# An image tower on one core: the causal attention's selection and softmax cut at the last visible key, and the last attention cut in two halves

## What is computed

```python
def L2_attn(x, Wq, Wk, Wv, Wo):            # the causal attention: 4 heads of 16
    scores = jnp.max(Q[:, :, :, None, :] + K[:, :, None, :, :], axis=-1)
    scores = jnp.where(causal_mask, -jnp.inf, scores)
    topk_vals, topk_idx = jax.lax.top_k(scores, 8)
    attn = jax.nn.softmax(topk_vals, axis=-1)
    ctx = jnp.einsum('bhtk,bhtkd->bhtd', attn, V gathered at topk_idx)
    return ctx @ Wo.T

def L3_attn(nodes, W):                     # the last attention: one head of 64
    x = jnp.einsum('bnf,fg->bng', nodes, W)
    prods = jnp.einsum('bnf,bmf->bnm', x, nodes)
    att_scores = jax.nn.softmax(prods / sqrt(64), axis=-1)
    return jnp.einsum('bnm,bmf->bnf', att_scores, nodes)
```

## Time and profile before

| | |
|---|---|
| Median of 3 runs | 168.89 us (168.25 to 169.76) |
| The profiled execution's own time | 169.38 us |
| Its span in the profile | 167.5 us |
| PE busy | 148.9 us (89%) |
| DVE busy | 102.5 us (61%) |
| ACT busy | 71.7 us (43%) |
| POOL busy | 32.3 us (19%) |
| PE's granted clock, mean | 0.988 |

### The profile page before, as it was taken

How to read it: one execution, slowest core, us unless ns; L and a number is a source line. 1 busy time by engine, 2 the same in 40 slices (tenths; PEclk the granted TensorE clock), 3 DMA queues, 4 the chain that set the end, 5 groups by cost and what they waited for, 6 DMA issues and landing times.

```text
span 167.5 us, 2891 instructions
## 1 busy us (share of the span) xinstructions
PE 148.9 (89%) x1122; PEld 72.0 (43%) x1122; DVE 102.5 (61%) x284; ACT 71.7 (43%) x133; POOL 32.3 (19%) x83
## 2 busy tenths in 40 slices
PE   6999889989997997988998896999799998999970
PEld 2446265534542352534543312466335454564420
DVE  7314876844657629487497799932868466213981
ACT  3736942756362010365430000615574056476523
POOL 7400000037778400001000000700039200000000
PEclk9999999999999999999999996999999999999999
DMA  5999960000000000000032000000000000000001
GB/s 171 328 429 319 301 244 0 4 0 2 2 6 0 0 0 0 0 4 0 0 56 54 0 0 2 0 4 0 0 4 0 0 0 4 0 0 4 2 0 35
DMA packets 4916, 8.26 MB, mean 49 GB/s; under 512 B 2747, under 2 KB 2875, under 8 KB 4774
## 3 DMA queue, kind: packets, MB, share of 16 engines
q1 hardware_dynamic: 4902, 8.07, 14.9%
HBM read 7.70 MB, written 0.37 MB: 48 GB/s over the span
## 4 chain that ended last, share of the span: by engine, by line
PE 60%; DVE 23%; ACT 8%; DMA 4%; issue 3%; POOL 0%; DVEq 0%; ACTq 0%; POOLq 0%
PE ps L386 9%; PE ps L445 8%; PE ps L432 7%; DVE scores L1280 5%; PE ps L793 5%; PE ps L439 4%; PE ps L393 3%; PE ps L400 3%; DMA k_scratch<-k_parts_tok 2%; DVE scores_rest L1299 2%; PE ps L536 2%; PE ps L544 2%; ACT hidden L855 2%; DMA k_parts_img<-k_scratch 2%; DVE hidden_gated L1090 1%
## 5 line engine op out<-in xcount | busy, mean ns | idle before, releaser
L386 PE MATMUL ps<-idle_operand 128*128 128x512 bf16 x153 | 42.8, 403 | 4.1 <-DVE scores L1280 1.7
L1090 DVE TENSOR_TENSOR hidden_gated<-hidden,ps 128x576 f32<-128x576 f32 x28 | 19.9, 751 | 10.3 <-PE ps L439 8.9
L855 ACT ACTIVATE hidden<-ps,weights_sb 128x576 f32<-128x576 f32 x28 | 19.5, 737 | 12.0 <-PE ps L432 9.5
L386 PEld LDWEIGHTS ps<-idle_operand 128*128 128x128 bf16 x153 | 13.5, 104 | 22.2 <-issue 6.2
L847 ACT ACT_TABLE_LOAD x16 | 20.5, 1283 | 0.3
L835 ACT ACTIVATE squares<-ps 128x288 f32<-128x288 f32 x8 | 3.3, 411 | 33.9 <-PE ps L445 9.2
L445 PE MATMUL ps<-hidden_gated,weights_sb 128*64 128x288 f32 x112 | 16.4, 419 | 0.0
L1029 DVE COPY centred<-ps 128x288 f32<-128x288 f32 x8 | 3.7, 457 | 17.2 <-ACT squares L835 17.2
L432 PE MATMUL ps<-h,weights_sb 64*128 64x288 f32 x80 | 13.0, 436 | 1.1 <-ACT hidden L855 0.8
L300 POOL CAST combine_parts_T<-combine_parts_T 48x288 f32<-48x288 bf16 x3 | 1.3, 421 | 65.2 <-DVE combine_parts_T L1061 65.2
L1280 DVE TENSOR_REDUCE scores<-ps 128x32 f32<-128x512 f32 (+1 forms) x15 | 8.8, 665 | 2.2 <-PE ps L679 2.2
(11 more groups left out here) (284 smaller groups left out, 231.9 us busy)
## 6 DMA issues: line engine op xcount, KB each, us to landing
patch_sb<-patches SPq DMA_DIRECT2D x6, 288.0 KB, 5.4
weights_sb<-weights SPq DMA_DIRECT2D x1, 1108.0 KB, 9.5
weights_sb<-weights SPq DMA_DIRECT2D x1, 717.0 KB, 14.5
weights_sb<-weights SPq DMA_DIRECT2D x1, 689.0 KB, 13.2
weights_sb<-weights SPq DMA_DIRECT2D x1, 640.0 KB, 7.2
weights_sb<-weights SPq DMA_DIRECT2D x1, 512.0 KB, 11.9
weights_sb<-weights SPq DMA_DIRECT2D x1, 394.0 KB, 12.9
weights_sb<-weights SPq DMA_DIRECT2D x1, 375.5 KB, 6.5
```

The costliest lines, as they stand in the source:

```text
L386: mm(PS[:, bank, :], idle_in[:, 0:P], idle_in[:, :], start=True, stop=True)
L855: act.activation(HR[:, at % RING, :, :], two(ZA if ch % 2 == 0 else ZB), func, bias=w(f"b1_{n}")[:, ch:ch + 1]).then_inc(S["act_out"], 1)
L1090: dve.tensor_tensor(HG[:, at % GRING, :, :], HR[:, at % RING, :, :], two(GATE_AT[n][ch]), ALU.mult)\
```

## The change

In the causal attention each query tile is now worked on up to its last visible key: 8, 16, 24, 32 and 40 columns in L1287 and L1299, and 24 and 40 columns in the two pieces of the subtraction, the exponential and the division. The first piece of the subtraction waits for the first 12 of the 20 selections only. The masking multiplication is in two instructions (tiles 0 to 2, tiles 3 and 4), and PE transposes the first three tiles behind the first of them. For the columns that are no longer written, POOL fills all of `probs` (1280 columns in place of 480) and all of `scores_rest` (800 columns, new) at the start.

In the last attention each step is cut by the half h: both matmul loops have h as the outer loop, and the reduction, subtraction, exponential, sum, multiplication and the four transposes of each half are single steps with semaphore counts of their own. The second half's transposed probabilities are copied by DVE, between its two pieces of weight centring, and the first half's by ACT. The fillers ahead of the transposes are 7 in place of 9, and behind them 1 in place of 4.

```diff
+        CUT = ((0, 3, 24), (3, QT, SPAD))
@@ POOL
-            fills = [... (PR[:, :, :, SPAD:64], 0.0), ...
+            fills = [... (PR[:, :, :, :], 0.0), ...
+                     (REP[:, :, :, :], NEG), (ss[:, :], 1.0)]
...
-            pool.wait_ge(S["topped"], QT * HEADS)
-            for a, b in cut:
+            for a, b, keys in CUT:
+                pool.wait_ge(S["topped"], b * HEADS)
                 (subtract, columns 0:keys)
@@ PE
-            pe.wait_ge(S["prob2"], 1)
-            for pair in range(2):
-                z = flat2(ZA if pair == 0 else ZB, QT * P)
-                for j in range(QT):
-                    last = pe.transpose(...)
-                last.then_inc(S["prob2_t"], 1)
+            for n, (a, b, _) in enumerate(CUT):
+                pe.wait_ge(S["prob2"], n + 1)
+                for pair in range(2):
+                    z = flat2(ZA if pair == 0 else ZB, QT * P)
+                    for j in range(a, b):
+                        last = pe.transpose(...)
+                    if n == 1:
+                        last.then_inc(S["prob2_t"], 1)
...
-            for b8 in range(PER):
-                r0 = (b8 % 2) * 64
-                for h in range(2):
+            for h in range(2):
+                for b8 in range(PER):
+                    r0 = (b8 % 2) * 64
                     last = mm(PS[r0:r0 + POS, ZA + h, ...], XT[rows(h), ...], HP[rows(h), ...], ...)
-            last.then_inc(S["s3_done"], 1)
-            idle(9, ZB)
-            pe.wait_ge(S["p3_ready"], 1)
+                last.then_inc(S["s3_done"], 1)
+            idle(7, ZB)
             pe.wait_ge(S["h3_copied"], 1)
-            z = flat2(ZB, 8 * P, POS)
-            for q in range(8):
-                last = pe.transpose(z[:, q * P:(q + 1) * P], E3[:, q, :], c("ident"))
-            last.then_inc(S["p3_t"], 1)
-            idle(4, G)
-            pe.wait_ge(S["p3_copied"], 1)
-            for b8 in range(PER):
-                r0 = (b8 % 2) * 64
-                for h in range(2):
+            for h in range(2):
+                pe.wait_ge(S["p3_ready"], h + 1)
+                for q in range(4):
+                    last = pe.transpose(PS[0:POS, ZB + h, ...], E3[:, 4 * h + q, :], c("ident"))
+                last.then_inc(S["p3_t"], 1)
+            idle(1, G)
+            for h in range(2):
+                pe.wait_ge(S[f"p3_copied{h}"], 1)
+                for b8 in range(PER):
+                    r0 = (b8 % 2) * 64
                     last = mm(PS[rows(h), YB, b8 * POS:(b8 + 1) * POS], HB[:, b8, rows(h)],
                               ET[:, 4 * h + b8 // 2, r0:r0 + POS], start=False, stop=True, ...)
@@ DVE
-                    dve.max(top[:, j, h, :], SC[:, j, h, :]).then_inc(S["topped"], 1)
+                    dve.max(top[:, j, h, :], SC[:, j, h, 0:8 * (j + 1)]).then_inc(S["topped"], 1)
...
+            for h in range(2):
+                dve.wait_ge(S["s3_done"], h + 1)
+                step(dve.tensor_reduce(half3(r3[0], h), s3(h), AX, ALU.max))
+            sync()
+            for h in range(2):
+                dve.tensor_tensor(half3(S3, h), s3(h), row3(r3[0], h), ALU.subtract).then_inc(S["exp3_in"], 1)
+            for h in range(2):
+                dve.wait_ge(S["exp3_out"], h + 1)
+                step(dve.tensor_reduce(half3(r3[1], h), half3(E3, h), AX, ALU.add))
+            sync()
             link(dve.reciprocal(r3[2][:, :], r3[1][:, :]))
+            for h in range(2):
+                dve.tensor_tensor(half3(E3, h), half3(E3, h), row3(r3[2], h), ALU.mult).then_inc(S["p3_ready"], 1)
...
+            centre_wd(0)
+            dve.wait_ge(S["p3_t"], 2)
+            dve.tensor_copy(ET[:, 4:8, :]..., PS[0:POS, ZB + 1, 0:4 * P]).then_inc(S["p3_copied1"], 1)
+            centre_wd(1)
```

More of the change, by code:

```diff
@@ L300, in gates32 @@
                 pool.tensor_copy(CTF[0:6 * E, :], CT3[0:6 * E, :]).then_inc(S["ctf_ready"], 1)
-            fills = [(eps[:, 0:1], EPS), (eps[:, 1:2], EPS * EPS), (ones[:, :], 1.0), (SC[:, :, :, :], NEG), (PR[:, :, :, SPAD:64], 0.0), (VB[:, :, :, :], 0.0),
+            fills = [(eps[:, 0:1], EPS), (eps[:, 1:2], EPS * EPS), (ones[:, :], 1.0), (SC[:, :, :, :], NEG), (PR[:, :, :, :], 0.0), (VB[:, :, :, :], 0.0),
                      (warm[:, :], 0.0), (rr[:, :], 1.0),
-                     (ss[:, :], 1.0)]
+                     (REP[:, :, :, :], NEG), (ss[:, :], 1.0)]
             for n, (t, value) in enumerate(fills):
@@ L354, in _ @@
             pool.tensor_scalar(WRG[:, :], w("Wr"), w("gam2"), None, ALU.mult).then_inc(S["wr_gam"], 1)
[L355 to L359 removed]
+            for a, b, keys in CUT:
+                pool.wait_ge(S["topped"], b * HEADS)
+                pool.tensor_tensor(SE[:, a:b, :, 0:keys].rearrange("p j h s -> p (j h) s"),
+                                   SC[:, a:b, :, 0:keys].rearrange("p j h s -> p (j h) s"),
                                    top[:, a:b, :, 0].rearrange("p j h -> p (j h)").unsqueeze(2)
[L361 removed]
+                                   .to_broadcast([P, (b - a) * HEADS, keys]), ALU.subtract).then_inc(S["sub2"], 1)
             pool.wait_ge(S["top_sum"], 1)
[L363 removed]
+            for n, (a, b, keys) in enumerate(CUT):
                 pool.wait_ge(S["exp2_out"], n + 1)
[L365 to L367 removed]
+                pool.tensor_tensor(SE[:, a:b, :, 0:keys].rearrange("p j h s -> p (j h) s"),
+                                   SE[:, a:b, :, 0:keys].rearrange("p j h s -> p (j h) s"),
+                                   d20[1][:, a * HEADS:b * HEADS].unsqueeze(2).to_broadcast([P, (b - a) * HEADS, keys]),
                                    ALU.mult).then_inc(S["norm2"], 1)
@@ L689, in _ @@
             idle(4, MB)
-            pe.wait_ge(S["prob2"], 1)
-            for pair in range(2):
-                z = flat2(ZA if pair == 0 else ZB, QT * P)
-                for j in range(QT):
-                    last = pe.transpose(z[:, j * P:(j + 1) * P],
-                                        PR[:, j, 2 * pair:2 * pair + 2, :].rearrange("p h s -> p (h s)"), c("ident"))
-                last.then_inc(S["prob2_t"], 1)
+            for n, (a, b, _) in enumerate(CUT):
[3 more added lines that the diff above has]
+                    for j in range(a, b):
+                        last = pe.transpose(z[:, j * P:(j + 1) * P],
+                                            PR[:, j, 2 * pair:2 * pair + 2, :].rearrange("p h s -> p (h s)"), c("ident"))
+                    if n == 1:
+                        last.then_inc(S["prob2_t"], 1)
             idle(3, MB)
@@ L921, in _ @@
             act.activation(TE[:, :, :, :], TE[:, :, :, :], ACT.Exp).then_inc(S["top_out"], 1)
-            for n, (a, b) in enumerate(((0, 3), (3, QT))):
+            for n, (a, b, keys) in enumerate(CUT):
                 act.wait_ge(S["sub2"], n + 1)
-                act.activation(SE[:, a:b, :, :], SE[:, a:b, :, :], ACT.Exp).then_inc(S["exp2_out"], 1)
+                act.activation(SE[:, a:b, :, 0:keys], SE[:, a:b, :, 0:keys], ACT.Exp).then_inc(S["exp2_out"], 1)
             table(ACT.Sqrt)
@@ L950, in _ @@
                .then_inc(S["h3_copied"], 1)
-            act.wait_ge(S["exp3_in"], 1)
-            act.activation(E3[:, :, :], S3[:, :, :], ACT.Exp, scale=float(D) ** -0.5).then_inc(S["exp3_out"], 1)
+            for h in range(2):
+                act.wait_ge(S["exp3_in"], h + 1)
+                act.activation(E3[:, 4 * h:4 * h + 4, :], S3[:, 4 * h:4 * h + 4, :], ACT.Exp, scale=float(D) ** -0.5)\
+                   .then_inc(S["exp3_out"], 1)
             table(ACT.Sqrt)
             act.wait_ge(S["p3_t"], 1)
-            act.activation(ET[:, :, :].rearrange("p q t -> p (q t)"), flat2(ZB, 8 * P, POS), ACT.Copy)\
-               .then_inc(S["p3_copied"], 1)
+            act.activation(ET[:, 0:4, :].rearrange("p q t -> p (q t)"), PS[0:POS, ZB, 0:4 * P], ACT.Copy)\
+               .then_inc(S["p3_copied0"], 1)
             square(7, "acc", 6)
@@ L1298, in _ @@
                 for h in range(HEADS):
-                    dve.match_replace(REP[:, j, h, :], top[:, j, h, :], SC[:, j, h, :], 3 * NEG)\
+                    dve.match_replace(REP[:, j, h, 0:8 * (j + 1)], top[:, j, h, :], SC[:, j, h, 0:8 * (j + 1)], 3 * NEG)\
                         .then_inc(S["replaced"], 1)
[L1301 to L1306, removed]
+            for n, (a, b, keys) in enumerate(CUT):
+                dve.wait_ge(S["replaced"], b * HEADS)
+                dve.wait_ge(S["norm2"], n + 1)
+                dve.scalar_tensor_tensor(PR[:, a:b, :, 0:keys].rearrange("p j h s -> p (j h) s"),
+                                         REP[:, a:b, :, 0:keys].rearrange("p j h s -> p (j h) s"), 3 * NEG,
+                                         SE[:, a:b, :, 0:keys].rearrange("p j h s -> p (j h) s"), ALU.is_equal, ALU.mult)\
+                   .then_inc(S["prob2"], 1)
             dve.wait_ge(S["prob2_t"], 1)
@@ L1326, in _ @@
             step(dve.tensor_reduce(wd_sums, w("Wd").rearrange("p (c d e) -> p c e d", c=2, e=E), AX, ALU.add))
```

(15 more changed lines are left out.)

6 lines of the change are left out of this document (5 added, 1 removed).

## The result

The changed kernel takes 168.24 us (median of 22 runs, 167.43 to 169.26) where the kernel before takes 169.26 us (22 runs, 168.25 to 171.73). The ratio is 0.9949, with a 95% interval of 0.9933 to 0.9966: 0.86 us faster, between 0.58 and 1.13. The two medians lie 1.02 us apart; ratio and interval are taken from the fast executions alone, the medians from all. The time is inside the predicted range, on the predicted side, and smaller than one per cent; the forecast was 0.49 us.

What follows compares the result with a forecast made beforehand. No engine's total decides; the dependency chain, six tenths PE's and a quarter DVE's, bounds the kernel. Gains of 0.44 us (causal attention) and 0.05 (last) make 0.49 us, so 168.4 us by the median, range 167.5 to 169.4.

Steps and rivals of the forecast that it cites:

- The value matmuls in one tile: Last attention: with h outside, records follow at 58 ns for 29, so the series takes 2.02 us.
- (a): Last attention's value matmuls: one tile keeps 29 ns a record, weight loads queued ahead; 167.6 us; chance 0.18.
- (b): Value matmuls: lone tile's weight load never overlaps, 89 ns a record, 169.4 us; chance 0.18, including anything from 62 ns.
- The way to the value matmuls: Last attention, from scores through transposes and copies: value matmuls start at 142.85, 0.95 us before today's 143.80.
- the 0.05 of the forecast: Last attention's whole gain: value matmuls end at 144.87 for today's 144.92, where the drawing promises 0.87 us.
- DVE's 0.67 us: Causal attention: narrower columns in selections and replacements save up to 0.67 us at 1.04 ns a column, at least nothing.
- the time of the 25 fillers: Causal attention: PE's fillers run on unchanged to 109.18, then transposes start, in place of 109.58 or so.
- rival (c): Last attention: PE's clock falls after a 0.9 us wait before the transposes; 170.4 us; chance 0.07.
- the 0.44: Causal attention's gain: 0.40 us from the fillers' end and some 0.04 from a gap; 0.15 were replacements no shorter.
- The sum: Both attentions: 0.44 + 0.05 = 0.49 us off, 168.89 for the profiled execution, 168.4 by the median.
- inner band: Whole kernel: 168.1 to 168.8 us, for 0.15 to 0.44 in the causal attention and 55 to 62 ns a record; chance 0.55.

Runs made afterwards that it cites:

- e5: The kernel before with one edit, the half h as outer loop of the value matmuls: 169.92 us, ratio 1.0038 against the kernel before.
- e3: The changed kernel, with value matmuls waiting for both copies and the half as inner loop again: 168.22 us, ratio 0.9948 against the kernel before.
- e4: The changed kernel, with the last attention cut by images 0 to 3 and 4 to 7, h inside: 167.38 us, ratio 0.9908 against the kernel before.
- e6: The kernel before plus the causal cut alone, selections and replacements over all 40 columns again: 168.82 us, ratio 0.9984 against the kernel before.
- e1: The kernel before plus the causal attention's part of the change alone: 168.29 us, ratio 0.9947 against the kernel before.
- e12: The changed kernel run again unaltered, for a second trace: 168.11 us, ratio 0.9943 against the kernel before.
- e2: The kernel before plus the last attention's halves alone, without the causal hunks and fills: 169.17 us, ratio 1.0001 against the kernel before.
- e9: The kernel before with the last attention cut by images alone: 168.01 us, ratio 0.9941 against the kernel before.
- e10: The kernel before with only the two larger POOL fills at the start: 169.01 us, ratio 0.9992 against the kernel before.
- e11: The changed kernel with 9 fillers for 7 ahead of the last attention's transposes, 2 for 1 behind: 168.67 us, ratio 0.9960 against the kernel before.

## Why the prediction was right, and where not

**The value matmuls in one tile: right.** The deciding term was 2.02 us for a series of 1.12, and it is 1.85 (e5, by itself). The rate was right as well: where one tile works alone a record takes 58 or 59 ns. The 0.17 us too much come from using it for all records: seven steps around the change of h go at 29 ns, which is 0.20 us for the 0.41 of the forecast, and the first step is 80 ns. The rule of the Trainium skill that was named with it (TensorEngine Tiling, Key Properties), that different tiles can load weights and multiply in parallel, fits what e3, e4 and e5 measured. That a lone tile then has no overlap at all was my addition, and 58 ns speak against it, since load and streaming one after the other were put at 89.

**Rivals (a) and (b) are out.** With the old rate the series would have been 1.12 us, and with a load that never overlaps 2.98. The second rule of the Trainium skill that was named (TensorE: Matmul & The Clock Gate, Part 3, The mechanism), read as weight loads that never overlap in the same row group, is not borne out by this series: priced from this kernel's rows it gave 89 ns a record, for 58 measured.

**The way to the value matmuls: the mechanism right, sizes off.** The forecast had them 0.95 us sooner, they came 1.11 sooner. The score matmuls with h outside took 0.64 us (0.76 in the forecast), the transposes began 3.02 us after the first score matmul (3.14), and the values 4.30 us after it (4.46). That is 0.16 us, and with the 0.17 of the series the last attention gained 0.39 us for the 0.05 of the forecast (to the rounding of the terms).

**The causal attention: one step failed.** DVE's 0.67 us were right (0.66, and e6 shows that they come from the widths). The step that failed is that the time of the 25 fillers is "fixed as long as the clock's fall and return are", with the fall taken as given because "nothing before 102.10 is touched". The fall there is not part of every execution: it is in 3 of the 14 traces (the kernel before, e3, e4), while the wait of 1.73 us ahead of the first filler, which rival (c) named as what came before it, is in all 14. Where it occurs (e3, e4) the fillers run through and the gain is 0.36 us, close to the 0.44; where it doesn't (the changed kernel, e1, e12) DVE is the bound and the gain is 0.82. With the causal attention as before it is 7.47 us with the fall (the kernel before) and 7.46 or 7.47 without it (e2, e5, e9, e10): that version waits for DVE either way. One trace of before could not tell the two apart.

**Rival (c) was the right thing with the wrong place and chance.** A fall came, behind the value matmuls and not ahead of them, at a cost of 1.37 or 1.38 us (4.42 against 3.05 and 3.04) in the profiled execution; I gave it 0.07, and a lower mean clock is in 10 of 22. The wait before the transposes, which I took as its cause, was not it: the fall is there with a wait of 0.32 us (e11) and absent with one of 0.75 (e12). Whether the long series in one tile makes it likelier stays open. It is not needed for a low mean clock: e3, whose series is short again, has 0.984 or less in 6 of its 12 executions, and e1, with the last attention as before, in none. But the mean counts every low stretch, also one at the kernel's end that costs nothing, and doesn't say where one lay.

**The sum.** With the clock up throughout, the stages give 0.82 + 0.06 + 0.39 = 1.27 us. If 10 of 22 executions pay the 1.04 us between the two groups of times, 0.47 is lost on average and 0.80 remains, for 0.86 measured. That is an estimate and not shown, since executions of the kernel before differ in their mean clock as well (0.987 to 0.998 beside e1). What is shown is that the causal cut alone gives all of the measured gain, and that the halves alone give none within 0.4 us.

**Where luck helped.** The measured 168.24 us lies in the forecast's inner band of 168.1 to 168.8, but that band was counted down from 168.89, the median of three executions; over 22 the kernel before is at 169.26. As a gain, 0.86 us lies beyond the 0.09 to 0.79 of that band. The forecast left out 0.38 us in the causal attention and 0.34 in the last, and by the estimate above falls of the clock took about 0.5 back.

## What to carry to other kernels

When a series of small matmuls is cut so that half of it can start sooner, cut along the dimension that keeps its array tiles taking turns: the cut along h gave back 0.73 us of the 1.11 it won, and along the images 0.07. Fillers on PE are work in the list: once the engine that they cover for gets faster, they are the next bound, and two fewer gave 0.43 us in the trace. Before a term of a sum is fixed by a stretch at the lower clock, look at more than one execution for whether that stretch is always there.

## What the runs showed of the hardware

Six of the 14 traces have PE's clock at its lower level (1.2 GHz) for about 3.4 us in the middle of the kernel: around 102 us in the kernel before, e3 and e4, and behind the last attention in the changed kernel, e2 and e11. The same kernel had it in one execution and not in another (the changed kernel and e12). It cost 1.38 us where PE was the bound, 0.45 us (7.10 and 6.65) where DVE's work lay beside it, and nothing in the causal attention of the kernel before, where DVE was the bound.

Small f32 matmuls with 64 weight columns follow each other at 58 ns in one tile of the array and at 29 ns when two tiles take turns, though each record is 223 ns long. Two selections over 40 columns follow each other 0.10 us apart, and two over 8 columns 0.07; over all 40 selections and replacements DVE loses 1.04 ns for each column taken away (0.67 us for 640).
